# Products of the upsampling and the second convolution on 64x64 tiles, two samples in one moving operand

## The reference

```python
# TYPES = ('same', 'upsample', 'same', 'downsample'), K = 3, 32 channels
s = style @ mw.T + mb
weight = SCALE * w * s[:, None, :, None]
demod = lax.rsqrt(jnp.sum(weight * weight, axis=(2, 3)) + EPS)
weight = weight * demod[:, :, None, None]          # a weight for each sample
# upsample:  transposed convolution with stride 2, then a blur (1, 3, 3, 1)
# downsample: a blur, then a convolution with stride 2
```

## Time and profile before

| | |
|---|---|
| three runs, median (lowest to highest) | 1237.67 us (1237.02 to 1241.85) |
| the profiled execution: span from first to last instruction | 1240.5 us; no other time of it is listed |
| TensorE busy | 1192.5 us (96%), 21528 matmul instructions and as many weight loads |
| VectorE, ScalarE, GpSimd busy | 42%, 29%, 44% |
| granted TensorE clock, mean | 0.992 |

### The profile page before, as it was taken

How to read it: one execution, slowest core, us unless ns; L and a number is a source line. 1 busy time by engine, 2 the same in 40 slices (tenths; PEclk the granted TensorE clock), 3 DMA queues, 4 the chain that set the end, 5 groups by cost and what they waited for, 6 DMA issues and landing times.

```text
span 1240.5 us, 46135 instructions
## 1 busy us (share of the span) xinstructions
PE 1192.5 (96%) x21528; PEld 705.2 (57%) x21528; DVE 519.5 (42%) x1010; ACT 356.9 (29%) x762; POOL 540.5 (44%) x411
## 2 busy tenths in 40 slices
PE   5898999999999999999999999999999999999997
PEld 4345565655565556655555556555565555565565
DVE  6862343443443434343344343444343333434343
ACT  2252243233232223123322222323222222313221
POOL 4656416555334446444155553355354333644400
PEclk9899999999999999999999999999999999999999
DMA  5533100020413000002123000002112000001001
GB/s 149 225 138 137 62 2 2 2 62 22 186 53 121 3 2 2 2 8 90 71 70 138 3 2 2 3 2 96 70 69 80 27 3 2 2 2 54 18 19 52
DMA packets 21454, 63.73 MB, mean 51 GB/s; under 512 B 4528, under 2 KB 5296, under 8 KB 17040
## 3 DMA queue, kind: packets, MB, share of 16 engines
q1 hardware_dynamic: 19488, 60.06, 13.3%
q10 hardware_dynamic: 1776, 0.73, 0.2%
HBM read 42.95 MB, written 17.83 MB: 49 GB/s over the span
## 4 chain that ended last, share of the span: by engine, by line
PE 88%; DVE 3%; issue 2%; DMA 0%; ACT 0%; DVEq 0%
PE bank_b L1311 27%; PE bank_a L117 13%; PE bank_a L104 11%; PE bank_b L104 11%; PE bank_b L87 8%; PE bank_a L1248 5%; PE bank_a L75 3%; PE bank_b L1269 3%; PE bank_b L1263 2%; PE bank_b L1323 2%; PE bank_b L1304 1%; DVE z L1154 1%; PE bank_b L1282 1%; PE bank_b L1292 1%; PE bank_b L1325 1%
## 5 line engine op out<-in xcount | busy, mean ns | idle before, releaser
L920 POOL TENSOR_TENSOR sum_v<-raw_v 128x768 f32<-128x768 f32 x30 | 55.3, 1845 | 581.7 <-ACT raw_v L978 581.7
L1311 PE MATMUL bank_b<-w_hi,y3t_hi 128*128 128x512 f32 x512 | 209.8, 410 | 1.8 <-issue 1.8
L1311 PE MATMUL bank_b<-w_lo,y3t_hi 128*128 128x512 f32 x512 | 203.8, 398 | 4.5 <-issue 4.5
L1311 PE MATMUL bank_b<-w_hi,y3t_lo 128*128 128x512 f32 x512 | 204.5, 399 | 0.0
L117 PE MATMUL bank_a<-y,w_down 64*32 64x512 f32 x3072 | 172.2, 590 | 0.0
L1104 DVE TENSOR_TENSOR x<-bank_b,x 128x512 f32<-128x512 f32 x96 | 66.4, 691 | 203.1 <-PE bank_b L1311 162.8
L972 ACT ACTIVATE y<-bank_a,cb,tab 128x512 f32<-128x512 f32 x64 | 49.6, 777 | 320.8 <-PE bank_a L117 315.7
L104 PE MATMUL bank_a<-y,wv 32*64 32x512 f32 (+2 forms) x3584 | 139.2, 476 | 1.8 <-issue 1.8
L104 PE MATMUL bank_b<-y,wv 32*64 32x512 f32 (+2 forms) x3584 | 138.3, 476 | 0.6 <-issue 0.6
L1311 PEld LDWEIGHTS bank_b<-w_hi,y3t_hi 128*128 128x128 f32 x512 | 97.9, 191 | 35.1 <-issue 13.4
L1311 PEld LDWEIGHTS bank_b<-w_hi,y3t_lo 128*128 128x128 f32 x512 | 97.5, 190 | 27.6 <-issue 4.7
(11 more groups left out here) (193 smaller groups left out, 1497.9 us busy)
## 6 DMA issues: line engine op xcount, KB each, us to landing
w_hi<-w_scratch SPq DMA_DIRECT2D x9, 1024.0 KB, 5.0
w_lo<-w_scratch SPq DMA_DIRECT2D x9, 1024.0 KB, 8.2
x_in<-in_x SPq DMA_DIRECT2D x32, 256.0 KB, 4.3
out_x<-out_tile SPq DMA_DIRECT2D x32, 256.0 KB, 2.4
w_raw<-in_w SPq DMA_DIRECT2D x3, 1024.0 KB, 6.3
w_scratch<-w_hi SPq DMA_DIRECT2D x3, 1024.0 KB, 3.9
w_scratch<-w_lo SPq DMA_DIRECT2D x3, 1024.0 KB, 6.9
w_raw<-w_scratch SPq DMA_DIRECT2D x2, 1024.0 KB, 10.1
```

Of the source, the lines that this page charges most:

```text
L920: ins = g_.tensor_tensor(dst[:, :, at:at + count].rearrange("p r k o -> p r (k o)"), src[:, :, 0:count].rearrange("p r k o -> p r (k o)"), ...
L1311: ins = pe.matmul(lin_ps[b][:], y3t[yi][:, k, P * b:P * (b + 1)], w[use(m) % 2][wi][:, k], start=(k == 0 and i == 0), stop=(k == KB - 1 an ...
```

## The change

Four samples in two neighbouring row groups become one 64x64 tile. The stationary operand gets 64 columns: the 32 output channels twice, once zero on the odd row groups and once zero on the even ones (the mask `halves`, applied on VectorE in setup). The moving operand holds two samples behind one another, so a tap has 2x96 columns and a ghost 2x32. One matmul now makes four samples' products, and a block has 20 matmuls in place of 80. A bank of each of two row halves takes both samples (`SPAN` = 224 columns each), so ScalarE copies two banks instead of four, each copy twice as large. The samples land in another order, for which `cond` is laid out a second way (four variants in place of two, 128 KB in place of 64). To make room, `bias_w` and the unmasked weights use the buffer of x, which is why GpSimd's first write to x waits for the bias matmuls, and `z_sum` uses `z_raw`.

```diff
     for s, at, first, count in (*((t, CH * t, 0, TAPS) for t in range(TAPS)),
                                 (TAPS, RAW * CH, TAPS - 1, 1), (TAPS + 1, (RAW + 1) * CH, 0, 1)):
-        for d in range(ROWS):
-            for r in range(ROWS):
-                rows, c = slice(CH * r, CH * (r + 1)), (r + d) % ROWS
-                last = pe.matmul(banks[r][CH * c:CH * (c + 1), at:at + count * CH], keep["up"][rows, l, s],
-                                 keep["w2s"][rows, (r + c) % ROWS, first * CH:(first + count) * CH],
+        for d in range(2):
+            for h in range(2):
+                rows, g = slice(2 * CH * h, 2 * CH * (h + 1)), (h + d) % 2
+                out = banks[h][2 * CH * g:2 * CH * (g + 1), 0:2 * SPAN].rearrange("p (j n) -> p j n", j=2)
+                last = pe.matmul(out[:, :, at:at + count * CH], keep["up"][rows, l, s].rearrange("p i o -> p (i o)"),
+                                 keep["w2s"][rows, 2 * g:2 * g + 2, first * CH:(first + count) * CH],
                                  start=(s == 0), stop=True, skip_group_check=True)
...
             pool.wait_ge(loaded["ob"], 16)
+            pool.wait_ge(bias_done, 1)
...
             dve.wait_ge(loaded["cw"], 16)
-            v.tensor_copy(keep["up"][:, :, 0:TAPS], cw[:, 1])
+            v.tensor_copy(up_one[:, :, 0:TAPS], cw[:, 1])
...
+            then(ins)
+            dve.wait_ge(loaded["halves"], 16)
+            for i in range(2):
+                ins = v.tensor_scalar(keep["up"][:, :, :, i].rearrange("p l s o -> p (l s) o"),
+                                      up_one.rearrange("p l s o -> p (l s) o"), halves[:, i:i + 1], None, ALU.mult)
             ins.then_inc(up_ready, 1)
...
             def products(n):
                 act.wait_ge(pr_done, n + 1)
                 act.wait_ge(wv_ready, n)
-                for r in range(ROWS):
-                    a.activation(raw_v[:, r, 1:RAW + 1].rearrange("p k o -> p (k o)"), bank_a[r][:, 0:RAW * CH],
-                                 ACT.Copy).then_inc(raw_ready, 1)
-                    a.activation(wv[:, r, TAPS_V:].rearrange("p k o -> p (k o)"),
-                                 bank_a[r][:, RAW * CH:(RAW + GHOSTS) * CH], ACT.Copy).then_inc(ghosts_ready, 1)
+                for h in range(2):
+                    pair = bank_a[h][:, 0:2 * SPAN].rearrange("p (j n) -> p j n", j=2)
+                    a.activation(raw_v[:, 2 * h:2 * h + 2, 1:RAW + 1].rearrange("p j k o -> p j (k o)"),
+                                 pair[:, :, 0:RAW * CH], ACT.Copy).then_inc(raw_ready, 1)
+                    a.activation(wv[:, 2 * h:2 * h + 2, TAPS_V:].rearrange("p j k o -> p j (k o)"),
+                                 pair[:, :, RAW * CH:SPAN], ACT.Copy).then_inc(ghosts_ready, 1)
```

More of the change, by code:

```diff
@@ L51 @@
 RAW, TAPS_V, GHOSTS = 2 * TAPS - 1, 2 * TAPS + 2, 2
+SPAN = (RAW + GHOSTS) * CH
 PAIRS_V = ((3, 0), (1, 1), (5, -1))
@@ L132, in setup_program @@
     GR = GROUPS * ROWS
-    cond = sb("cond", [STYLE, ROWS, 2, GR])
+    cond = sb("cond", [STYLE, ROWS, 4, GR])
+    halves = sb("halves", [P, 2])
     cond_v = sb("cond_v", [STYLE, ROWS, 2, GR])
@@ L196, in setup_program @@
     w0_ps = [*bank_a[2:4], *bank_a[0:2]]
-    names = ("ob", "cond", "cond_v", "mod_w", "mod_b", "conv_b", "cw", "coeffs", "scales", "b0", "a0", "w0",
+    names = ("ob", "halves", "cond", "cond_v", "mod_w", "mod_b", "conv_b", "cw", "coeffs", "scales", "b0", "a0", "w0",
              "gate", "delta", "a2", "b2", "a1", "r1", "b1", "a3", "b3", "as2", "bs2", "w2")
@@ L238, in _ @@
                 ("cond", cond[:], io["cond"]), ("cond_v", cond_v[:], io["cond_v"]), ("mod_w", mod_w[:], io["mod_w"]), ("mod_b", mod_b[:], io["mod_b"]),
-                ("cw", cw[:], io["cw"]), ("conv_b", conv_b[:], io["conv_b"]),
+                ("cw", cw[:], io["cw"]), ("halves", halves[:], io["halves"]), ("conv_b", conv_b[:], io["conv_b"]),
             ):
@@ L622, in _ @@
                 for g in range(ROWS):
+                    pair = 2 if q % CONVS in (1, 2) else 0
                     last = pe.matmul(mod_ps[q // 8][CH * g:CH * (g + 1), q % 8].rearrange("p o s -> p (o s)"), mod_w[:, q],
-                                     cond[:, g].rearrange("s o f -> s (o f)"), start=True, stop=True)
+                                     cond[:, g, pair:pair + 2].rearrange("s o f -> s (o f)"), start=True, stop=True)
             pe.wait_ge(loaded["cond_v"], 16)
@@ L912, in blurred @@
             def blurred(n):
-                pool.wait_ge(raw_ready, tiles(n, ROWS))
+                pool.wait_ge(raw_ready, evacuated(n))
                 chain_ = ((raw_v, sum_v[0], 1), (sum_v[0], sum_v[1], 1), (sum_v[1], wv, 0))
@@ L1230, in conv2 @@
                     pe.wait_ge(wv_ready, n + 1)
-                    pe.wait_ge(ghosts_ready, tiles(n, ROWS))
+                    pe.wait_ge(ghosts_ready, evacuated(n))
                 elif n:
@@ L1238, in down @@
                 if n + 1 < PHASES:
-                    pe.wait_ge(raw_ready, tiles(n + 1, ROWS))
-                    pe.wait_ge(ghosts_ready, tiles(n + 1, ROWS))
+                    pe.wait_ge(raw_ready, evacuated(n + 1))
+                    pe.wait_ge(ghosts_ready, evacuated(n + 1))
                 down_tiles(pe, bank_a, keep, layer(n), u).then_inc(dn_done, 1)
@@ L1473, in host_layout @@
     cond_v = cond[:, :, (b_v - at) % ROWS, b_v + 0 * at].transpose(0, 2, 3, 1, 4)
-    cond = np.stack([cond.transpose(0, 2, 1, 3), cond_t.transpose(0, 2, 1, 3)], axis=2)
+    pair, half = at[:, None] // 2, at[:, None] % 2
+    row_p = 2 * pair + at[None, :] % 2
+    col_p = (row_p + at[None, :] // 2 * 2 + half) % ROWS
+    cond_p = cond[:, :, row_p, col_p]
+    cond = np.stack([a.transpose(0, 2, 1, 3) for a in (cond, cond_t, cond_p, cond_t)], axis=2)
     w_do = [i["L0_ffn_W"].T, i["L1_ffn_W_base"].T, i["L2_ffn_kernel"], i["L3_ffn_W_up"].T]
@@ L1484, in host_layout @@
         "x": x,
-        "cond": cond.reshape(STYLE, ROWS, 2, GROUPS * ROWS),
+        "cond": cond.reshape(STYLE, ROWS, 4, GROUPS * ROWS),
+        "halves": np.tile(np.repeat(np.eye(2, dtype=np.float32), CH, axis=0), (2, 1)),
         "cond_v": np.repeat(cond_v, 2, axis=1).reshape(STYLE, ROWS, 2, GROUPS * ROWS),
```

36 lines of the change are left out of this document (20 added, 16 removed).

## The result

| | before | after |
|---|---|---|
| median of four runs (lowest to highest) | 1238.88 us (1237.02 to 1241.85) | 1206.94 us (1206.07 to 1208.1) |
| ratio, 95% interval | | 0.9734 [0.9715, 0.9752] |
| span of the profiled execution | 1240.5 us | 1206.3 us |

Faster by 2.7%. In each run of the changed kernel the time is 1.8 to 1.9 us above its own span.

A forecast was written before the change was run, and what follows sets the result against it. TensorE's own sequence was taken as the bound (busy 1192.5 of 1240.5 us). 1240.5 - 9.5 (block) - 13.6 (gaps) - 4.5 (clock) + 1.8 (setup) = 1214.7, stated as 1214 us; range 1206 to 1231.

The forecast's parts named there:

- The shorter block: Products on TensorE: a block takes 1.37 us instead of 1.78, gaining 0.41 in 23 blocks, -9.5 us (bounds 2.3 and 13).
- the cause of the gaps at the products: TensorE's idle gaps at the products are code that did not arrive in time, because dense blocks eat instructions too fast.
- the term of the gaps: TensorE's idle gaps at and right after the products go, less 1.5 us returning: -13.6 us (bounds 0 and 15.1).
- no shorter block: Rival: weight loads or round starts hold the new block up, so only the gaps go; 1222 to 1226 us, chance 0.12.
- taking turns: Rival: column tiles sharing 64 rows stream one after the other, block 2.59 us, 1244 us in all; chance 0.04.
- the gaps stay: Rival: gaps come from the queue, not the density of instructions, and only move; 1230 to 1233 us, chance 0.20.
- I let 1.5 us come back in other places: Allowance for new gaps at the convolutions, taking the gap gain from 15.1 to 13.6 us.
- the clock: Three stretches at half clock behind gaps go with them, 1.5 us each: -4.5 us (0 to 4.5).
- VectorE's queue is the path here: Setup: two masks on VectorE (1.5 us) delay what TensorE waits for, with cond's 0.3: +1.8 us (1.1 to 3.3).
- Not streaming: Old block of 1.78 us is paced by handing over instructions, about 10.5 ns each; streaming would be 0.61 us.
- Evacuation: 0: ScalarE's four larger copies a block instead of eight cost 0, since their readers come microseconds later.
- The shift of 2.8 us: Median of runs, 1237.67 us, lies 2.8 under the profiled span; differences between executions were put down most likely to gaps.

The follow-up runs named there:

- the spread experiment: Kernel before, with the products of the 16 plain phases spread in five steps between halves of the linear products; 1320.46 us, ratio 1.0639.
- twice the columns: Kernel before, each 32x32 product matmul streaming its operand twice (192 and 64 columns), same number of instructions; 1245.59 us, ratio 1.0029.
- the short fillers: Changed kernel with 60 one-column matmuls put ahead of each block of products, giving its old 320 instructions again; 1255.03 us, ratio 1.0118.

## Where the prediction was right, and where it was wrong

The shorter block and the cause of the gaps at the products were right, and the size was not. The step that failed is the term of the gaps: -13.6 us in the sum, 20.0 measured, above the bound of 15.1 that the prediction had set for it.

**Right: the block.** 1.78 to 1.36 or 1.37 us, full gain in plain phases and in layer 3, none in layer 1, where the gate wait went from 4.2 to 8.0 us (about 7.5 predicted). The rivals "no shorter block" and "taking turns" fell with it.

**Right: the cause of the gaps at the products.** Same packets at a slow pace, no gaps there; other instructions at the old pace, gaps at the same count; and each gap ends 1.2 to 1.6 us after a packet of code has landed. The rival "the gaps stay" fell. The packets also give an estimate of the pace that code can keep. In the kernel before, the next packet starts 1.1 to 1.5 us after the end of a gap, takes 0.9 to 1.6 us, and 1.2 to 1.6 us pass from its landing to the end of the next gap: some 3.5 us a packet. A block of 320 instructions in 1.78 us eats a packet in 1.4 us. So a gap should need a packet that lies nearly whole inside a block. Indeed all nine gaps at or right behind the products stand 118 to 161 matmuls after the start of their block, where a packet is some 127, so that most of the thirty blocks should have none.

By the Trainium skill, page "Runtime: NRT & Kernel Launch", section "Instruction fetch mechanics", code comes in blocks of 256 instructions, and crossing a block's border is mostly hidden. The first agrees here (7680 instructions fewer, 30 packets fewer). The second agrees by count (12 gaps in the main program, 169 packets in all) and not by cost: 18.1 us of idle time before, 0.8 after. The measurement decides.

**Wrong: the size of the gap term.** The step was "I let 1.5 us come back in other places: -13.6 us". The gaps at the products went as forecast, all 15.7 us. But nothing came back: at the second convolution 2.4 us became 0.8, where 1.5 more had been allowed for (3.1 us of difference). The experiments show that these gaps do not follow the pace of the block (0.5 to 3.8 us in the table, 2.2 with the slowest block). Two things fit the traces: they stand on packet borders, which fall on other instructions when the count changes, and data transfers hold much of the DMA engines before each of them. No run tests this, so why this kernel has so few stays open, and that they fell was luck.

The other 3.3 us is that a gap costs more than its idle time. The waits named issue fell by 17.3 us, of which 0.6 went to the gate in phase 19, as forecast; from start to start it is 20.0. Idle time counts from the end of the last instruction, and without a gap the next one starts before that end. At 140.06 the idle time is 1.51 us, but the two products around it start 1.70 apart, where 0.01 is usual. At 130.10 it is 1.37 us, and the half of the second convolution that holds it takes 6.65 us (128.21 to 134.86) in place of 4.22. Together this is 6.4 of the 8.4 us that the span is shorter than my sum; setup is 1.8, the block 0.2, and the clock came out at its 4.5.

**Wrong: setup.** The step was "VectorE's queue is the path here", +1.8 us; TensorE's second half of the w0 products started at 39.12, before at 39.53. The timeline of setup before, ScalarE and VectorE:

```profile
19.86 2.19 ACTq L298 DMA_DIRECT2D eb<-in_eb  x1
...
22.57 1.28 ACT L302 ACT_TABLE_LOAD   x1 [8.66 <-issue]
22.71 0.27 DVE L540 TENSOR_SCALAR var<-bank_b 128x128 f32<-128x128 f32 x1
23.86 0.74 ACT L302 ACTIVATE mod_sq<-var 128x640 f32<-128x640 f32 x1
```

The same after, VectorE:

```profile
15.57 2.46 DVE L528 TENSOR_SCALAR w_up<-x,halves 128x640 f32<-128x640 f32 x2
...
23.43 0.28 DVE L553 TENSOR_SCALAR var<-bank_b 128x128 f32<-128x128 f32 x1
```

And ScalarE:

```profile
23.75 0.74 ACT L308 ACTIVATE mod_sq<-var 128x640 f32<-128x640 f32 x1 [2.23 <-DVE var L553]
```

Before, the variances were ready at 22.98, but the root waited for ScalarE's own queue: one DMA issue of 2.19 us, then the table load until 23.85. In the trace after, that issue took 0.45 us, and the root follows the variances. So VectorE had 0.87 us of cover, and the masks took 2.46 us (I said 1.5) but moved the variances by only 0.73: `cw` landed 0.3 earlier, where 0.3 later was predicted, and the instructions behind got shorter (three at L540, 1.33 us where it was 2.20), since they now run later, most of them after GpSimd has scaled x (14.30 to 18.92); the masks done twice bear that reason out for the masks (1.14 to 1.32 us beside it, 0.54 after it). In the trace of the spread experiment, whose setup is the old one, the issue took 0.45 us too and the root began at 22.94; against that one the new root is 0.8 us late, and VectorE's queue was the path there. With twice the columns, the old setup again, the issue behind it took 1.90 us and the root began at 23.97. So the step holds in one execution of the old setup and fails in two. The 0.4 us itself is no measure of the change: with the old setup the main program started at 80.17, 81.30 and 81.91 us in three executions, and half-clock stretches in setup differ between them. What makes an issue slow stays open.

**Half right: what paced the old block.** "Not streaming" was wrong in part: twice the columns cost 0.58 us, all of the streaming, a third of the block. The sum did not rest on it, because the new block was worked out from its own streaming.

**A cover that was thinner than I said.** "Evacuation: 0" held, since the block now ends earlier; but the spread experiment shows that products later by a few microseconds already make TensorE wait up to 3.9 us.

**The shift of 2.8 us** between span and median was misread: time and span of one run differ by less than 2 us the other way, so the profiled execution was one of the longer runs.

## What to carry to other kernels

Divide the instructions of a dense stage by its time: here 320 in 1.78 us cost 15.7 us of idle time at and behind the products and 4.5 in clock over 30 blocks, more than twice what the shorter block itself brought, and 80 in 1.37 us cost nothing there. Tiles twice as large, half of them zeros, with two samples in one operand, were worth it here for that reason alone. And when a block before a wait gets shorter, start earlier what the wait is for: six linear products' worth of order took away the 8.0 us that TensorE had waited.

## What I had not expected of the hardware

- A gap sits at a fixed count of instructions: after 155 of the same block in three kernels with different instructions and times. By the count of 256 to a packet one can tell which blocks may break off.
- Small rounds cost more than their columns: some 0.1 us for each round of sixteen 32x32 tiles (0.58 of 1.78 us is streaming), and 0.38 us for 40 more passes on 64x64 tiles, while 40 passes of twice the columns ran at their streaming time (1.22 us by estimate, 1.36 measured with 0.15 of entry and exit).
- Length alone does not say after which gap the clock falls. In the kernel before the granted clock was 0.50 for some 3.4 us after gaps of 4.48, 2.03 and 1.84 us and not after one of 1.94 (1014.77); with the short fillers it was after 0.88 us (145.07). Windows of the kernel before, after its gaps of 1.94, 2.03 and 1.84 us (the clock is third from the end):

```profile
1016.80:1020.20 3.40, 3.40 (x20) 2.79 (x20) 0.21 (x1) 1.36 (x8) 1.85 (x1) 1.00 0.03 5
...
763.00:766.40 3.40, 3.40 (x9) 2.65 (x8) 0.69 (x1) 3.07 (x9) 2.82 (x2) 0.50 0.02 5
981.40:984.80 3.40, 3.40 (x9) 2.66 (x9) 0.00 (x0) 0.00 (x0) 3.24 (x3) 0.50 0.02 5
```

- A mask of 128x640 on VectorE took 1.23 us beside GpSimd, and 0.54 once GpSimd was done; 128x480 alone took 0.41. By the Trainium skill, page "GPSIMD Engine Reference", section "Key points", the two engines share SBUF interfaces, with contention for some forms of VectorE's instructions. The durations agree; which form these masks have, no run here shows.
